# In the head of an attention and experts kernel: gate rows sent ahead of copies of ones, five more unread products, and the first quad's picks in another order

## What is computed

```
igate, fgate = concat[q, k, v] @ ig_kernel + ig_bias, ... @ fg_kernel + fg_bias
cums = cumsum(log_sigmoid(fgate))                     # called F in the kernel
log_D = cums[t] - cums[s] + igate[s]   (s <= t);  max_log_D = max over s
C = (q @ k.T / 8) * exp(log_D - max_log_D)
h = C / (max(|sum C|, exp(-max_log_D)) + 1e-6) @ v    # then normalized per head
x = x + h * outnorm_weight
...
n1 = _ln(x, ln1_g, ln1_b)
q, kk, v = projections of n1 by mha_wq, mha_wk, mha_wv        # M = 2, H = 16, KD = 16
attn = softmax(q @ kk.T / 4);  ctx = attn @ v                 # mixed by mha_probs
n2 = _ln(x, ln2_g, ln2_b);  top 2 of 8 experts: gelu(n2 @ sw1) @ sw2
```

## Time and profile before

| | us |
|---|---|
| median of three runs | 1461.99 |
| the profiled execution | 1459.95 |
| its span on the core | 1458.2 |
| TensorE busy | 1409.4 (97%) |
| VectorE busy | 1108.9 (76%) |
| ScalarE busy | 901.4 (62%) |
| GpSimd busy | 366.9 (25%) |

### The profile page before, as it was taken

The page is one execution under the profiler, slowest core; times in us unless marked ns, Lnnn a source line. Parts: engine busy times, 40 slices in busy tenths (PEclk is TensorE's granted clock), DMA queues, the critical chain, the costliest instruction groups (busy, mean ns, idle before and its releaser), DMA issues.

```text
span 1458.2 us, 22355 instructions
## 1 busy us (share of the span) xinstructions
PE 1409.4 (97%) x7754; PEld 732.4 (50%) x7754; DVE 1108.9 (76%) x2300; ACT 901.4 (62%) x1675; POOL 366.9 (25%) x351
## 2 busy tenths in 40 slices
PE   8998899999999999999999999999999999999999
PEld 5643434455445554555544554445545555454356
DVE  4678877987779776998769877797868887687721
ACT  3246566775667656676566756676566665657752
POOL 6421134205113051122412152130511323112000
PEclk9899999999999999999999999999999999999999
DMA  4052335421623317241354305333073322552002
GB/s 101 30 66 59 39 44 93 76 52 30 100 54 74 67 27 119 46 91 41 44 98 77 60 30 87 66 74 67 16 102 73 71 58 37 77 66 60 15 2 87
DMA packets 92308, 90.17 MB, mean 62 GB/s; under 512 B 16482, under 2 KB 87266, under 8 KB 91294
## 3 DMA queue, kind: packets, MB, share of 16 engines
q1 hardware_dynamic: 92196, 88.73, 34.7%
HBM read 35.05 MB, written 4.25 MB: 27 GB/s over the span
## 4 chain that ended last, share of the span: by engine, by line
PE 82%; issue 7%; DVE 6%; SPq 1%; ACT 1%; POOL 1%; DMA 0%; DVEq 0%; POOLq 0%; ACTq 0%
PE psum L817 14%; PE psum L802 14%; PE psum L787 13%; PE psum L646 7%; PE psum L774 7%; PE psum L755 7%; PE psum L429 5%; PE psum L452 4%; DVE mx L1290 3%; PE psum L678 3%; PE psum L532 2%; PE psum L630 2%; PE psum L542 1%; SPq L1835 1%; DVE qbuf L1064 1%
## 5 line engine op out<-in xcount | busy, mean ns | idle before, releaser
L1577 ACT ACTIVATE prob<-psum 128x512 f32<-128x512 f32 x1024 | 565.1, 601 | 290.0 <-PE psum L817 174.5
L1290 DVE TENSOR_REDUCE mx<-psum 128x1 f32<-128x512 f32 x1024 | 642.5, 680 | 98.8 <-PE psum L787 97.3
L802 PE MATMUL psum<-qst,kst 98*128 98x512 bf16 x1024 | 354.8, 383 | 6.4 <-ACT prob L1577 3.0
L787 PE MATMUL psum<-kst,qst 96*128 96x512 bf16 x1024 | 316.7, 381 | 4.5 <-issue 1.8
L817 PE MATMUL psum<-prob,vst 128*17 128x512 f32 x2048 | 247.1, 599 | 0.7 <-ACT prob L1577 0.6
L802 PEld LDWEIGHTS psum<-qst,kst 98*128 98x128 bf16 x1024 | 98.2, 99 | 203.0 <-issue 120.1
L787 PEld LDWEIGHTS psum<-kst,qst 96*128 96x128 bf16 x1024 | 99.8, 98 | 123.8 <-issue 16.9
L817 PEld LDWEIGHTS psum<-prob,vst 128*17 128x17 f32 x2048 | 46.2, 97 | 131.2 <-issue 104.3
L1726 POOL CAST parts<-resid 128x512 bf16<-128x512 f32 x64 | 39.5, 617 | 286.6 <-DVE resid L1172 286.6
L774 PE MATMUL psum<-w,cxT 128*128 128x256 f32 x448 | 104.6, 379 | 0.0
L755 PE MATMUL psum<-n2T,x 128*128 128x512 f32 x224 | 100.7, 592 | 0.0
(11 more groups left out here) (231 smaller groups left out, 1745.3 us busy)
## 6 DMA issues: line engine op xcount, KB each, us to landing
kst<-parts SPq DMA_DIRECT2D x186, 128.0 KB, 4.6
qst<-parts SPq DMA_DIRECT2D x186, 128.0 KB, 4.9
cmat<-G_dram SPq DMA_DIRECT2D x7, 1024.0 KB, 4.6
x<-in_L_ffn_fw SPq DMA_DIRECT2D x14, 512.0 KB, 3.6
w<-in_L_ffn_fw SPq DMA_DIRECT2D x14, 512.0 KB, 3.9
xbuf<-in_x SPq DMA_DIRECT2D x8, 512.0 KB, 4.6
kin<-in_ctx SPq DMA_DIRECT2D x8, 512.0 KB, 3.8
out<-acc SPq DMA_DIRECT2D x7, 512.0 KB, 3.8
```

What stands on the lines that cost most here:

```text
L787: e.matmul(psum[:, u.bank, :], qst[0:KROWS, h, t * P:(t + 1) * P], kst[0:KROWS, h, :], start=True, stop=True).then_inc(u.full, 1)
L802: e.matmul(psum[:, u.bank, :], kst[0:KROWS + 2, h, g * P:(g + 1) * P], qst[0:KROWS + 2, h, :], start=True, stop=True).then_inc(u.full, 1)
L1290: e.tensor_reduce(mx[:, qq * QUAD + j, t:t + 1], psum[:, u.bank, :], AX, ALU.max).then_inc(u.free, 1)
L1577: e.activation(prob[:, g % 2, j, :], psum[:, u.bank, :], ACT.Exp).then_inc(u.free, 1)
```

## The change

Three edits, all in the head. SP steps through its stage A up to the move of gi before it sends the copies of ones. The filler after the gate products has 20 products where it had 18, and a new filler of 3 stands between the bank taken for `num0` and the waits of `num0`. The picks of the first quad are no longer all of k and then all of q: hi, mid of k, hi of q for three heads, lo of k, mid and lo of q for the same three, and then the fourth q head alone.

```
@@ TensorE, stage_a
                 if b == 0:
-                    keep_clock(18)
+                    keep_clock(20)
...
                     u = take("num", b, c)
+                    if b == 0 and c == 0:
+                        keep_clock(3)
                     if c == 0:
...
                         e.wait_ge(choice_made, 2)
-                        for which in range(2):
-                            pick(which, range(QUAD))
+                        pick_first()
...
+            def pick_first():
+
+                us = {}
+                heads = (range(QUAD), range(QUAD - 1))
+                for which, j in ((0, 0), (0, 1), (1, 0), (0, 2), (1, 1), (1, 2)):
+                    e.wait_ge((split_hi, split_mid, split_lo)[j], which + 1)
+                    for h in heads[which]:
+                        if j == 0:
+                            us[which, h] = take("pick", which, h)
+                        u = us[which, h]
+                        ins = e.matmul(psum[0:KROWS, u.bank, :], chosen[:, which, j, h, :], parts[:, which, j, :],
+                                       start=j == 0, stop=j == 2)
+                        if j == 2:
+                            ins.then_inc(u.full, 1)
+                pick(1, [QUAD - 1])
@@ SP
+            first = Side(stage_a(0), defaultdict(lambda: 0, ctx=-1, x=-1, gi=-1))
+            first.upto(-1)
             e.wait_ge(ones, 1)
             for i in range(1, M * H // HC):
                 e.dma_start(kst[KROWS:KROWS + 2, i * HC:(i + 1) * HC, :], kst[KROWS:KROWS + 2, 0:HC, :]).then_inc(ones_in, 16)
-            for _ in stage_a(0):
-                pass
+            first.rest()
```

## The result

| | before | changed |
|---|---|---|
| median of seven executions, us | 1466.79 | 1455.78 |
| lowest and highest | 1460.44, 1467.85 | 1454.33, 1458.84 |
| ratio, 95% interval | | 0.9938, 0.9918 to 0.9959 |
| profiled execution, us | 1459.95 | 1455.78 |
| its span, us | 1458.2 | 1454.1 |

The changed kernel is faster by 0.6%; 1456.7 was forecast and 1455.78 measured. Four more executions of the kernel before had moved its own median from 1461.99 to 1466.79, so part of the 11 us between the medians is the scatter of seven executions. In two later sessions, on two chips, the ratio was 0.9960 (0.9946 to 0.9975) and 0.9956 (0.9940 to 0.9973), which is 5.4 and 5.9 us between the medians. Over all sessions 22 executions of the changed kernel have a median of 1456.8 and 93 of the kernel before one of 1463.0: 6.2 us, 0.42%.

A forecast was written before the change was run, and what follows sets the result against it. TensorE, busy 97% of the span, was taken to bound the kernel through idles and low clock in the head. 0.90 + 3.45 + 0.30 + 0.10 + 0.60 = 5.35 us off 1461.99 gave 1456.7; range 1451.5 to 1463.0.

The forecast's parts named there:

- The gates' rows: Head: gi sent ahead of the ones lets `g` start at 20.28 in place of 21.18, 0.90 us earlier.
- (e): Rival at the gates: the rows of gi don't land earlier, 0.90 us less gain, 1457.6 us; chance 0.06.
- The two products and the clock behind them: First filler: two more products leave 0.13 us of idle; clock staying at 2.4 GHz past 25.84 gives 3.45 us.
- Rival (b): Filling the idles doesn't keep the clock up, because short products around them matter; gain 0.6 us, 1461.4 us; chance 0.11.
- The three products: Before `num0`: they fill the wait, adding at most 0.1 us; faster `cross` products bring the gain from 4.35 to 4.65.
- VectorE leads from there: From the `cross` products to normalization: VectorE sets the pace, most low clock is hidden, normalized rows start at 53.5.
- The new idles: Before `fold`: 1.95 us of new idle, then low clock for 2.6 to 5.3 us, hidden but for 0.4 at most.
- (a): Rival: the clock falls over the projections, where nothing hides it; 1458.4 us, up to 1460.1; chance 0.23.
- The picks: First quad: the new order fills the wait for k's low part; 0.6 us, bounds 0.3 and 0.9.
- the list of signs: Trace times that would show the forecast right or wrong, among them first maxima near 64.4.
- rival (c): Behind the head, later clock falls go or come elsewhere: 1453.7 or 1459.7 us; chance 0.14, better side likelier.
- (d): Slower: clock stays low from the idle before `fold` through filler and projections, 1467.9 us; loss from about 16 us low; chance 0.04.

The follow-up runs named there:

- the fillers' trace: Kernel before with only the fillers of 20 and 3 products added, gi still behind the ones, picks as before; 1461.68 us, 0.9990 to the kernel before.
- the old picks: Changed kernel with the first quad's picks in the old order, all of k and then all of q; 1459.79 us, 0.9970 to the kernel before.
- the fold wait filled: Changed kernel with three more unread products ahead of the `fold` products and 23 in place of 20 behind; 1456.65 us (0.9943), repeated 1459.03 us (0.9981).

## Why the prediction was right, step by step

- **The gates' rows.** `g` moved by 0.87 (0.90 forecast) and lost its wait for the transfer. The value lies also in something I had not counted: SP's issues and the transfer itself vary, and with gi behind the ones each delay is on the path, 1.2 us in the fillers' trace. With gi ahead a small delay is hidden, since `g` waits for F anyway, but not every one: with the old picks gi was issued at 18.13 in place of 17.38, and `g` is at 20.76 in place of 20.31. (e) did not occur: `g` is at 20.3 to 20.8 in all eleven traces with gi ahead, and at 21.2, 21.2 and 22.4 in the three with it behind.
- **The two products and the clock behind them.** Forecast 3.45 on top, measured 4.41 from 33.05 to 28.64 in all, against 4.35. The size is right, and is the difference of two traces; the mechanism was told too simply, and that this pair met the sum so closely is partly luck. The clock also falls there with almost no idle, for 3.4 us, and that costs 1.7. The gain at the weighing is 4.4 against the worst case of before and 2.7 against the other one. In the trace with the gates' rows and the picks alone the clock stayed up without the two products, so the 3.45 us can't be put down to them; that they make the fall rarer isn't shown. Rival (b), given 0.11, is true in part: the clock can fall behind the short products with no idle ahead of them, and doesn't each time.
- **The three products.** `num0` at 32.98 (33.0 forecast), the use of the `cross` products at 35.67 (35.7). But my value for them, 0.3 and 0.1, rests on the one trace in which the low stretch began late and ended early. In the four other traces without them, weighing to first pick is 32.8, so 1.7 is what they save as a rule. The rows hinted at this: the filler ended 0.4 us behind the first of the four normalized rows, so a longer low stretch would show.
- **VectorE leads from there.** Normalized rows at 53.44 (53.5). Borne out by the fold wait filled, which changed nothing.
- **The new idles.** 1.55 before `fold` (1.95 forecast; the `num` chain ends later than I summed), then low for 3.4 us (2.6 to 5.3), filler to 53.2 (52.8 to 54.2). (a), the clock falling over the projections, is in none of the nine traces with the filler before `num0`.
- **The picks.** 0.66 (0.6), the steadiest of the three edits.
- **Behind the head.** 5.36 at the first maxima (64.94; the list of signs says 64.4, which the sum, 70.30 less 5.35, doesn't give) and 4.1 in the span. The starts of L1327 against L1310 tell where it went: 6.3 us ahead at the first quad, since the low stretch of the earlier trace rows is 3.4 us long and not 6.8; 6.6 until the 17th; 5.3 from the 18th, where TensorE waits for a transfer that in the first trace of before was there in time; 5.5 at the last; and 1.4 given back after it, where the row 1414.40:1417.60 above is low and nothing before answers to it. That is rival (c), both ways at once. It isn't shown to be the doing of the change: the second trace of the kernel before has a low stretch of 3.4 us there too, at 115, a wait of 0.7 us for the same transfer, and a stretch of 3.4 us at the lower clock at 1419. The wait, in the changed kernel from 452 to 453:

```profile
PE psum L819 <- DMA qst<-mrow: 1.2, 1, 1.2
```

- **Slower**, (d): the low stretch behind the new idle never passed 3.4 us in a kernel with the three products, where the 16 us of (d) were needed; the longest in any head was 13.7.
- **The chances.** The first measurement lies over the 0.5% that I called the limit, and the two later ones under it; 0.76 for within it and 0.21 for faster fit that, as far as three measurements can tell. The times resolve little below the whole: alone, the gates' rows stand clear of 1 (0.9975) and the fillers don't (0.9990), and the picks were not run alone. Each of the four kernels that lack one part or two of the change (0.9957 to 0.9972) has an interval that overlaps the changed kernel's. What the three products and the picks save is shown by traces, not by times; for the two products neither shows it.

## What to carry to other kernels

Ahead of a chain in which TensorE mostly waits, count not only how long it stands but what it does around the wait: unread products of 256 columns in a wait of 1.7 us kept the clock up in nine traces of nine, and are free up to the moment at which the awaited operand is there. Check first which engine leads behind them, since low clock beside a leading VectorE cost nothing here. And take a second trace of the kernel before, before a gain is sized: here the price of the same idle was 0.3 us in one trace and 1.7 in four others.

## What the hardware showed that I had not expected

- The clock fell to 1.2 GHz with TensorE busy in 3.37 and in 3.15 of the 3.40 us ahead, some 1.8 us of them in short products of four columns; with 3.38 us busy in the same instructions it stayed at 2.4 GHz.
- The low stretches in the heads were 3.4, 6.8, 10.2 or 13.7 us long. For the same instructions of the kernel before they were 6.8 and 10.2 us in one execution and 3.4 and 13.7 in another.
- The mean granted clock goes along with most of the scatter of a kernel: over 76 executions 1.5 us per 0.001 of mean granted clock, from 1456.9 to 1467.5 us.
- The same two loads took from 0.98 to 1.55 us of SP's time to issue, and the rows of gi behind them took 2.04 us from issue to use in one trace and 2.66 in another.
